# Layer 1's linear attention: the taps of queries and keys as shifted multiply-adds on VectorE, over one raw projection

## What is computed

```python
def short_conv(x, w):                      # w: [channels, 4]
    xp = pad(x, 3 zero tokens in front)
    y = x
    for j in range(4):
        y = y + xp[:, j:j + l, :] * w[:, j]
    return y
h = layernorm(x)
q = l2norm(silu(short_conv(h @ Wq.T, conv_q)))   # per head of 8 channels
k = l2norm(silu(short_conv(h @ Wk.T, conv_k)))
v = silu(short_conv(h @ Wv.T, conv_v))
o = per head: q @ W0 + tril(q @ k.T) @ v
o = layernorm over each head's 8 channels (gamma, beta)
x = x + (o * (h @ Wg.T)) @ Wo.T
```

## Time and profile before

| What | Value |
|---|---|
| Median of 3 runs | 3837.25 us (3829.97 to 3837.67) |
| The profiled execution's own time | 3835.66 us |
| Its span, first to last instruction | 3833.8 us |
| Mean granted TensorE clock | 0.962 |
| Busy share of the span | PE 90%, DVE 70%, ACT 64%, POOL 54% |
| First and last query and key product of this block | 1193.2 and 1404.4 us |

### The profile page before, as it was taken

How to read it: one execution, slowest core, us unless ns; L and a number is a source line. 1 busy time by engine, 2 the same in 40 slices (tenths; PEclk the granted TensorE clock), 3 DMA queues, 4 the chain that set the end, 5 groups by cost and what they waited for, 6 DMA issues and landing times. The chain is left out here.

```text
span 3833.8 us, 90102 instructions
## 1 busy us (share of the span) xinstructions
PE 3465.1 (90%) x30069; PEld 2574.1 (67%) x30069; DVE 2688.0 (70%) x5870; ACT 2437.2 (64%) x9595; POOL 2075.0 (54%) x2606
## 2 busy tenths in 40 slices
PE   8989979988988999999889998899899998788897
PEld 5656645557776878888666665666688874456587
DVE  6857749977774767777688886644577754979822
ACT  6958944445452437777635991455688875688655
POOL 4534319977993433344366540275666635556744
PEclk9989999999999999999989998999999999999889
DMA  7013420010000000000000003135500003300078
GB/s 110 2 23 48 53 61 1 1 56 1 1 1 22 2 2 7 6 7 6 6 2 6 12 7 119 28 99 91 220 22 21 22 30 116 116 2 10 31 263 302
DMA packets 320103, 185.17 MB, mean 48 GB/s; under 512 B 214104, under 2 KB 289127, under 8 KB 318613
## 3 DMA queue, kind: packets, MB, share of 16 engines
q1 hardware_dynamic: 303716, 147.68, 14.2%
q0 software_dynamic: 13568, 27.36, 3.1%
q10 hardware_dynamic: 2370, 4.39, 0.3%
HBM read 131.43 MB, written 50.54 MB: 47 GB/s over the span
## 5 line engine op out<-in xcount | busy, mean ns | idle before, releaser
L3889 POOL DMA_INDIRECT l2f_b_xb<-l2f_tokens,l2f_inv x160 | 155.5, 972 | 174.8 <-issue 157.9
L2684 POOL TENSOR_TENSOR l1x_Sx<-l1x_Sx,l1x_sm 128x512 f32<-128x512 f32 x128 | 132.6, 1046 | 184.7 <-DVE l1x_sm L2890 184.7
L2684 POOL TENSOR_TENSOR l3a_Sx<-l3a_Sx,l3a_sm 128x512 f32<-128x512 f32 x128 | 133.4, 1043 | 129.8 <-DVE l3a_sm L2890 128.2
L3005 ACT ACTIVATE l1x_Sx<-l1x_Sx,l1x_nmx 128x128 f32<-128x128 f32 x512 | 199.0, 393 | 3.8 <-DVE l1x_nmx L2884 3.8
L1470 PEld LDWEIGHTS l0f_acc<-l0f_d_xk,l0f_d_Z 128*128 128x128 f32 x1024 | 124.7, 191 | 113.8 <-POOL l0f_d_Z L1438 112.8
L3005 ACT ACTIVATE l3a_Sx<-l3a_Sx,l3a_nmx 128x128 f32<-128x128 f32 x512 | 199.0, 392 | 0.1
L865 ACT ACTIVATE l3f_Pr<-l3f_S,l3f_nmx 128x128 f32<-128x128 f32 x512 | 182.5, 402 | 3.3 <-DVE l3f_nmx L795 3.3
L865 ACT ACTIVATE l2x_Pr<-l2x_S,l2x_nmx 128x128 f32<-128x128 f32 x512 | 183.9, 426 | 0.4 <-DVE l2x_nmx L795 0.4
L1350 ACT ACTIVATE l0x_Pr<-l0x_S,l0x_nmx 128x128 f32<-128x128 f32 x512 | 181.4, 403 | 3.1 <-DVE l0x_nmx L1267 2.6
L865 ACT ACTIVATE l0a_Pr<-l0a_S,l0a_nmx 128x128 f32<-128x128 f32 x512 | 182.6, 406 | 0.7 <-DVE l0a_nmx L795 0.7
L1470 PE MATMUL l0f_acc<-l0f_d_xk,l0f_d_Z 128*128 128x128 f32 x1024 | 144.5, 284 | 25.1 <-POOL l0f_d_Z L1438 24.9
(11 more groups left out here) (757 smaller groups left out, 11938.7 us busy)
## 6 DMA issues: line engine op xcount, KB each, us to landing
l3f_b_W<-in_l3f_we SPq DMA_DIRECT2D x72, 514.0 KB, 5.5
l3f_sorted<-l3a_blank SPq DMA_DIRECT2D x1, 17680.0 KB, 51.1
l3x_Mb<-l3x_dram_max SPq DMA_DIRECT2D x32, 512.0 KB, 4.3
l2f_results<-l2f_b_ys SPq DMA_DIRECT2D x40, 256.0 KB, 2.8
l2f_W<-in_l2f_w SPq DMA_DIRECT2D x1, 6144.0 KB, 25.9
l3f_b_xb<-l3f_sorted SPq DMA_DIRECT2D x72, 65.0 KB, 4.4
l0f_ew<-in_l0f_ew SPq DMA_DIRECT2D x1, 4096.0 KB, 13.2
l3f_XS<-l3f_results SPq DMA_DIRECT2D x8, 512.0 KB, 6.6
```

The source lines that it names most:

```text
L2684: pool.tensor_tensor(quad(Sx, s, q), quad(Sx, s, q), bcast_in(sm[:, s, 4 * q:4 * q + 4], P), ALU.mult).then_inc(w_done, 1)
L3005: ins = nc.scalar.activation(Sx[:, s, h, :], Sx[:, s, h, :], ACT.Exp, bias=nmx[:, s, h:h + 1], accum_out=sm[:, s, h:h + 1])
L3889: pool.indirect_dma_start(xb[:, j % 16, :], None, rows[:, :], bass.IndirectOffsetOnAxis(inv[:, j:j + 1], 0), bounds_check=None).then_inc(x ...
```

## The change

Queries and keys get one product each instead of four, over the untapped weights `wq` and `wk`. ACT then does three operations (`keep_raw`): it copies both raw projections to `raw`, which has three zero columns in front of each, and writes the current token's term, scaled by a column of weights (the last tap plus one), to `cv`. DVE adds the three earlier taps (`convolve`): for queries and then for keys, three multiply-adds each, over `raw` from column j on, with a per-partition weight read from memory, where each waits for the one before it. `silu_qk` reads `cv` instead of bank A. Values keep their four products. The layer norm, its transpose and the projection of queries and keys move one step ahead, so the loops begin one step earlier, and `xb` has three buffers. The tap weights come by one more small DMA, and one more DVE operation in the setup adds the one.

```diff
+    xb = sb("xb", [P, 3, 3 + P])
+    raw = sb("raw", [P, 2, 2, 3 + P])
+    cv = sb("cv", [P, 2, 2, P])
...
+    def convolve(eng, ops, b, n, done):
+        wait(eng, raw_done, b + 1)
+        acc = cv[:, b % 2, n, :]
+        for j in (2, 1, 0):
+            wait(eng, done, 3 * b + 2 - j)
+            ops.scalar_tensor_tensor(acc, raw[:, b % 2, n, j:j + P], cols[:, n, j:j + 1], acc, ALU.mult, ALU.add).then_inc(done, 1)
...
         def project_qk(b, n):
             wait(pe, xb_done, b + 1)
-            wait(pe, qkt_done, b)
+            wait(pe, raw_done, b)
...
-            for j in range(4):
-                mm = nc.tensor.matmul(A[:, cols], taps[:, j, cols], xb[:, b % 2, j:j + P],
-                                      start=(j == 0), stop=(j == 3))
+            mm = nc.tensor.matmul(A[:, n * P:(n + 1) * P], (wq, wk)[n], xb[:, b % 3, 3:3 + P], start=True, stop=True)
...
-            if span(b + 2):
-                project_qk(b + 2, 0)
+            if span(b + 3):
+                project_qk(b + 3, 0)
...
-            if span(b + 3):
-                normed_T(b + 3)
+            if span(b + 4):
+                normed_T(b + 4)
...
-                ln.moments_of(nc, dve, b + 4, b % 2, X)
+            if span(b + 5):
+                wait(dve, ln.offset_done, b + 4)
+                ln.moments_of(nc, dve, b + 5, (b + 1) % 2, X)
...
             if b >= -1 and (span(b - 1) or span(b + 1)):
                 roots(b - 1)
+            if span(b + 3):
+                convolve(dve, nc.vector, b + 3, 0, conv_q)
+                convolve(dve, nc.vector, b + 3, 1, conv_k)
+        nc.vector.memset(raw[:, :, :, 0:3], 0.0)
...
+        def keep_raw(b):
+            wait(act, qk_mm, b + 1)
+            wait(act, qkt_done, b - 1)
+            wait(act, conv_q, 3 * b - 3)
+            wait(act, conv_k, 3 * b - 3)
+            for n in range(2):
+                nc.scalar.activation(cv[:, b % 2, n, :], A[:, n * P:(n + 1) * P], ACT.Identity, scale=cols[:, n, 3:4])
+            nc.scalar.copy(raw[:, b % 2, :, 3:3 + P], A[:, 0:2 * P].rearrange("p (n t) -> p n t", n=2)).then_inc(raw_done, 1)
...
         def silu_qk(b):
-            wait(act, qk_mm, b + 1)
-            nc.scalar.activation(qkT[:, b % 4, :], A[:, 0:2 * P], ACT.Silu).then_inc(qkt_done, 1)
+            wait(act, conv_q, 3 * b + 3)
+            wait(act, conv_k, 3 * b + 3)
+            nc.scalar.activation(qkT[:, b % 4, :], cv[:, b % 2, :, :].rearrange("p n t -> p (n t)"), ACT.Silu).then_inc(qkt_done, 1)
...
                 square_centred(b - 1)
+            if span(b + 3):
+                keep_raw(b + 3)
...
+                sp.dma_start(cc[:, :, :], d["l1a_cc"]).then_inc(w_in, 16)
-                dve.wait_ge(w_in, 64)
+                dve.wait_ge(w_in, 80)
+                nc.vector.tensor_scalar(cc[:, :, 3], cc[:, :, 3], 1.0, 0.0, ALU.add, ALU.add)
```

More of the change, by code:

```diff
@@ L1931, in delta_attention @@
      v_done, qexp_done, s_mm, p_done, pv_mm, ot_done, cen_mm, osq_done, rt_mm, rt_done, u_done,
-     wide_done, g_done, y_mm, x_done) = sems(27)
+     wide_done, g_done, y_mm, x_done, raw_done, conv_q, conv_k) = sems(30)
     ln.sems(sems)
+    def convolve(eng, ops, b, n, done):
[4 more added lines that the diff above has]
+            ops.scalar_tensor_tensor(acc, raw[:, b % 2, n, j:j + P], cols[:, n, j:j + 1], acc, ALU.mult, ALU.add).then_inc(done, 1)
     def gpsimd(pool):
@@ L1964, in step @@
                 gated(b - 2)
[L1965 to L1968, removed]
+            if span(b + 5):
+                wait(pool, ln.done, b + 4)
+                ln.rstd(pool, b + 5, (b + 1) % 2, C)
+                ln.offset(pool, b + 5, (b + 1) % 2)
         return step
@@ L2035, in project_v @@
             for j in range(4):
-                nc.tensor.matmul(B[:, 0:P], xb[:, b % 2, j:j + P], taps[:, j, 2 * P:3 * P],
+                nc.tensor.matmul(B[:, 0:P], xb[:, b % 3, j:j + P], taps[:, j, 2 * P:3 * P],
                                  start=(j == 0), stop=(j == 3))
-            nc.tensor.matmul(B[:, P:2 * P], wg, xb[:, b % 2, 3:3 + P], start=True, stop=True).then_inc(vg_mm, 1)
+            nc.tensor.matmul(B[:, P:2 * P], wg, xb[:, b % 3, 3:3 + P], start=True, stop=True).then_inc(vg_mm, 1)
         def normed_T(b):
             wait(pe, ln.done, b + 1)
-            wait(pe, qkt_done, b)
+            wait(pe, raw_done, b)
             nc.tensor.transpose(A[:, 2 * P:3 * P], ln.xn[:, b % 2, :], C.ident).then_inc(xnt_mm, 1)
@@ L2051, in step @@
                 sum_keys(b - 1)
-            if span(b + 2):
-                project_qk(b + 2, 0)
+            if span(b + 3):
+                project_qk(b + 3, 0)
             if span(b - 1):
                 centre(b - 1)
-            if span(b + 2):
-                project_qk(b + 2, 1)
+            if span(b + 3):
+                project_qk(b + 3, 1)
             if b >= -1 and (span(b - 1) or span(b + 1)):
@@ L2121, in step @@
                 mask(b, 1)
-            if span(b + 4):
-                wait(dve, ln.offset_done, b + 3)
-                ln.moments_of(nc, dve, b + 4, b % 2, X)
+            if span(b + 5):
+                wait(dve, ln.offset_done, b + 4)
+                ln.moments_of(nc, dve, b + 5, (b + 1) % 2, X)
             if span(b - 2):
@@ L2171, in copy_normed @@
         def copy_normed(b):
-            wait(act, vg_mm, b - 1)
+            wait(act, vg_mm, b - 2)
             wait(act, xnt_mm, b + 1)
-            nc.scalar.copy(xb[:, b % 2, 3:3 + P], A[:, 2 * P:3 * P]).then_inc(xb_done, 1)
+            nc.scalar.copy(xb[:, b % 3, 3:3 + P], A[:, 2 * P:3 * P]).then_inc(xb_done, 1)
         def step(b):
@@ L2178, in step @@
                 copy_scale(b - 2)
[L2179 to L2180 removed]
+            if span(b + 4):
+                ln.apply(nc, act, b + 4, b % 2, X, xnt_mm)
             if span(b - 1):
@@ L2189, in step @@
                 silu_v(b + 2)
-            if span(b + 3):
-                copy_normed(b + 3)
+            if span(b + 4):
+                copy_normed(b + 4)
         return step
@@ L2194, in delta_attention @@
                  gpsimd=gpsimd, tensor=tensor, vector=vector, scalar=scalar, S=S, x_done=x_done,
-                 banks={"S0": ((p_done, 2 * NB - 1),), "S1": ((p_done, 2 * NB),), "A": ((qkt_done, NB), (xb_done, NB)),
+                 banks={"S0": ((p_done, 2 * NB - 1),), "S1": ((p_done, 2 * NB),), "A": ((raw_done, NB), (xb_done, NB)),
                         "B": ((vs_done, NB),), "O": ((ot_done, NB), (x_done, NB)), "Y": ((u_done, NB), (rt_done, NB), (osq_done, NB), (r_done, NB + 2))})
@@ L3222, in _ @@
                 steps = delta.gpsimd(pool), wide.gpsimd(pool), phi.gpsimd(pool), heads.gpsimd(pool)
-                for n in range(-4, HEADS + NB + 2):
+                for n in range(-5, HEADS + NB + 2):
                     steps[0](n)
@@ L3249, in _ @@
                 hold_clock(nc, C, delta.S, 3)
-                for n in range(-3, HEADS + NB + 2):
+                for n in range(-5, HEADS + NB + 2):
                     steps[0](n)
@@ L3301, in _ @@
                 steps = delta.scalar(act), wide.scalar(act), phi.scalar(act), heads.scalar(act)
-                for n in range(-4, HEADS + NB + 1):
+                for n in range(-5, HEADS + NB + 1):
                     steps[0](n)
@@ L4634, in arrange @@
     a["l1a_conv"] = np.concatenate([v["L1_attn_conv_" + n] for n in "qkv"]).T.reshape(-1)
+    a["l1a_cc"] = cols([v["L1_attn_conv_" + n].reshape(P, 4) for n in "qk"])
     blocks = np.zeros((16, 8, 16, 8), np.float32)
```

8 lines of the change are left out of this document (4 added, 4 removed).

## The result

The changed kernel takes 3897.55 us in the median of 4 runs (3883.55 to 3904.40), against 3837.46 us: a ratio of 1.0149, with a 95% interval of 1.0130 to 1.0168, so 50 to 64 us slower. The forecast was slower, at 3866 us with a range up to 3884. The direction was right, but the loss came out twice as large as forecast (60.1 us between the medians, against 30.5), and the median lies 14 us beyond the upper end of the range.

What follows compares the result with a forecast made beforehand. PE sets the step before, but the loop through PE and DVE decides: 23.5 (loop) + 3.0 (filling and emptying) + 4 (clock) = 30.5 us on 3835.66 gives 3866 us, slower by 0.8%; range 3848 to 3884.

Steps and rivals of the forecast that it cites:

- Loop, without collision: 27 steps from step 2: loop through DVE and PE takes 7.78 us a step instead of 6.91, 23.5 us more.
- Clock: PE's waits at low clock add 0.77 us to a step; taken for one step in five, +4 us.
- Filling and emptying: Block's ends: +1 us filling, +2.07 from step 0 to 1, +0.6 in step 1, -0.7 in step 29; together +3.0 us.
- What bounds it before, and the loop after: PE sets 6.91 us a step before; afterwards the loop through both engines decides, 7.78 us, DVE waiting 0.55 before the addition.
- 0.87 us of gaps a step: On PE, removed products had hidden ACT's squaring and copy to `oT`; gaps of 0.44 and 0.43 us open.
- 4 x 0.383 + 2 x 0.27 = 2.07 us a step: DVE's six multiply-adds: four dependent start distances of 0.383 us and two independent of 0.27, 2.07 us a step.
- chain of four: Existing DVE multiply-adds of the same form, 1.50 us from first start to last end, used to price the six.
- rival 4: Clock falls in nearly every step, each low stretch adding 0.77 us to the loop: 3883 us; chance 0.14.
- Covered costs: ACT's `keep_raw`, 1.1 us a step, and the layer norm's move cost nothing; setup put at 0.1 us.
- The dependence: On DVE, waiting on the instruction just ahead costs 0.11 us; by the skill's rule the forecast would be 12 us lower.
- Rivals 1 to 3: Smaller loss, 3849 to 3852 us, chance 0.15; no change, some 3839, chance 0.05; faster, 3824, chance 0.04.
- listed signs of being wrong: No PE idle before `centre`, multiply-adds 0.32 us apart or less, DVE waiting for `raw_done`, or stretch clock under 0.8.

Runs made afterwards that it cites:

- with spreading moved: Changed kernel, but POOL's spreading of the queries waits until DVE's six multiply-adds are through: median step 7.78 us, 27 steps 214.53 us.
- the removal alone: Changed kernel without its six multiply-adds on DVE; ACT's three operations and the single products stay: step 6.35 us, 27 steps 171.63 us.
- the immediate number: Changed kernel with 0.125 in the six multiply-adds in place of a per-partition weight read from memory: shortest step 8.21 us.
- The alternation: Changed kernel with POOL's spreading late, plus multiply-adds alternating between queries and keys: step 7.41 us rather than 7.78.
- the filling products: Changed kernel with six extra unread products per step in PE's idle time ahead of the centring product: 27 steps 230.1 us.
- the first keys-only version: Changed kernel, queries' four products back on PE, late spreading, division ahead of masks, values' products ahead of centring: step 7.35 us, 27 steps 198.47 us.

## Why the prediction was half right

The terms of its sum, for the block, against what the runs showed:

| Term | Forecast, us | Measured, us |
|---|---|---|
| Loop, without collision | 23.5 | 23.5 (27 x (7.78 - 6.91), with spreading moved) |
| Collision of POOL and DVE | none | 17.8 (27 x (8.44 - 7.78)) |
| Clock | 4 | 11.5 |
| Filling and emptying | 3.0 | 5.7 |
| Sum | 30.5 | 58.5 |

- **What bounds it before, and the loop after.** Right, with the six multiply-adds left aside. The work that DVE gained does not fit into DVE's idle time, because that is in front of the addition. Mask to addition, the wait of 0.5 us and PE's wait ahead of the centring came where they were written; the price of PE's relief, 0.87 us of gaps a step, fits the removal alone as a sum (6.35 us against 5.57 + 0.87 = 6.44).
- **The step that failed: the six multiply-adds at "4 x 0.383 + 2 x 0.27 = 2.07 us a step".** They took 2.79, and 27 times the collision is 17.8 us, the largest part of the 28 us that the sum was short on the block. The row of the chain of four has the form but not the company: beside it POOL issued an indirect DMA (so it did for 124 of the 128 multiply-adds of the earlier trace rows, of which none took over 402 ns), and ran no tensor operation. I looked for a row with the same operands and did not ask what runs on POOL in that place of the step. The answer was in the code and in the trace of before: POOL's `unit_keys` waits for `roots`, `spread` follows it, and the multiply-adds follow `roots` too. The Trainium skill states the rule (SBUF — State Buffer, section "Who interferes with whom"): a VectorE instruction with two SBUF inputs contends with a GpSimd instruction that reads SBUF. This case agrees: 1.01 us instead of 0.35, and 1.02 with the immediate number instead of 0.28.
- **The clock: "one in five".** This was mis-sized too: 11.5 us, not 4. In the steps of 8.44 us PE waits 2.18 us ahead of the centring, not the 1.8 of the forecast; in the steps of 7.78 us it waits 1.51 us. With the waits of the shorter step (7.78 us) the clock cost 214.53 - 27 x 7.78 = 4.5 us, close to the 4 that I took; so most of this miss goes with the collision. Eleven of the 27 steps held a low piece, where the forecast had five or six and rival 4 had all; a low piece cost 1.0 us rather than 0.77, with the five slightly longer steps behind slow ones counted in. The Trainium skill (TensorE: Matmul & The Clock Gate, section "HAM oscillation — how this bites in real kernels") describes a loop whose clock falls again in every pass. This trace agrees that a wait in each step slows it again and again, but not in every step.
- **Filling.** +3.2 to the first mask instead of 1; +3.5 for the first two steps instead of 2.7, which again has the collision in it; -1.0 for the end instead of -0.7 (by the prediction's own 6.44 and 6.91 us a step that term would be -0.5).
- **Covered costs.** `keep_raw` took 0.88 us on ACT (two copies together 0.62 us, then one of 0.38), off the path as said. DVE waits for it only while the pipeline fills.
- **The dependence.** The rows priced a wait for the instruction just ahead at 0.11 us. The alternation shows 0.12 us at the three places that POOL does not touch, so the rows were the right choice.
- **The range** ended at 3884, where it was set by the clock falling in every step. It had no term for a multiply-add that is longer than its row. Rivals 1 to 3 fell with it, all of them on the side of a cheaper DVE. None of the listed signs of being wrong came: PE was idle ahead of the centring, and the clock was 0.84. PE's busy share (83%) and the clock lay outside what was forecast (75 to 80%, 0.9 to 1.0), and so did the multiply-add of 1.01 us, where all were to be 0.35 us long.

What stays open: why the clock still fell four times with the filling products, which cost the last 2 us of that run, though PE waited 0.88 us in every step of the first keys-only version and kept a clock of 1.00; and whether the PSUM operand is what spares the mask.

## What to carry to other kernels

Price an added instruction by what runs beside it as much as by its form: look up what the other engines do in that place of the step, and whether two of them read SBUF at the same time. Then walk the path once round from an instruction to itself a step later; an operation's place on that path (a 0.28 us division, 11 us in all) can be worth more than the work moved between engines. Work taken off the engine that sets the pace is worth only what the next wait leaves of it, and a TensorE left waiting may lose its clock too.

## What the runs showed of the hardware beyond what was expected

- A VectorE multiply-add with both tensors in SBUF took 1014 ns beside a POOL instruction of 1.09 us, 352 ns alone, and in all 31 cases ended 0.14 to 0.15 us behind it. POOL's own went from 1.04 to 1.09 us. A mask with one operand in PSUM took 1.22 us beside the same POOL instruction, before the change and with the spreading moved.
- A weight per partition read from memory costs a 128x128 multiply-add 0.06 us (342 against 283 ns).
- A VectorE multiply-add that waits for the one just ahead starts 0.12 us later than one that waits for the one before that (0.38 against 0.26 us from start to start).
- Left idle for 2.18 us of 8.44 ahead of the centring, TensorE ran at the low clock for 75.5 of 239.35 us; with that wait partly filled (0.83 us left), for 13.7 of 230.09.
